# Gated delta-rule heads on one core: decay rows by DMA, tail decay on the keys, fillers in halves, a new order of a head step

## The reference

```python
mixed = silu(causal_conv(hidden @ w_qkv, conv_w))        # kernel of 4 taps
q, k, v = split(mixed)                                   # 16 key heads, 32 value heads, 128 wide
beta = sigmoid(hidden @ w_b)
g = -exp(A_log) * softplus(hidden @ w_a + dt_bias)
qf, kf = l2norm(q) * 128 ** -0.5, l2norm(k)
def step(state, t):
    state = state * exp(g_t)
    delta = (v_t - k_t @ state) * beta_t
    state = state + outer(k_t, delta)
    return state, q_t @ state
o = o * silu(z);  o = rmsnorm(o) * gamma;  return o @ w_out
```

## Time and profile before

| | us |
|---|---|
| median of 3 runs | 1450.89 |
| profiled execution, time | 1452.2 |
| profiled execution, span | 1450.4 |
| head steps (first to last state copy, 16 copies) | 102.4 to 996.8 |
| a full head step (120.67 us for two, 403.7 to 524.4) | 60.3 |
| PE busy of 119.0 us of full steps | 113.53 |
| DVE, ACT, POOL busy of the same | 93.52, 80.08, 82.18 |

### The profile page before, as it was taken

How to read it: one execution, slowest core, us unless ns; L and a number is a source line. 1 busy time by engine, 2 the same in 40 slices (tenths; PEclk the granted TensorE clock), 3 DMA queues, 4 the chain that set the end, 5 groups by cost and what they waited for, 6 DMA issues and landing times. The chain is left out here.

```text
span 1450.4 us, 24932 instructions
## 1 busy us (share of the span) xinstructions
PE 1304.9 (90%) x8680; PEld 872.4 (60%) x8680; DVE 962.6 (66%) x1918; ACT 792.2 (55%) x1944; POOL 750.8 (52%) x1245
## 2 busy tenths in 40 slices
PE   6768999999999999999999999988898899899893
PEld 4356666666666666666666666665545466545672
DVE  5847778787787877878778787774602366641454
ACT  3546676666766667666666666665432365420120
POOL 1675776857758667585676856761000000117363
PEclk9969999999999999999999999999999999999997
DMA  2534355354453544535445354364201950202687
GB/s 81 134 64 114 64 152 142 90 150 113 133 138 93 150 117 128 143 88 150 117 129 143 88 150 117 114 145 157 66 0 27 374 160 1 81 13 104 137 185 185
DMA packets 233180, 171.71 MB, mean 118 GB/s; under 512 B 163746, under 2 KB 202998, under 8 KB 230240
## 3 DMA queue, kind: packets, MB, share of 16 engines
q1 hardware_dynamic: 226912, 161.59, 41.3%
q0 software_dynamic: 6144, 8.53, 3.3%
HBM read 104.64 MB, written 65.83 MB: 118 GB/s over the span
## 5 line engine op out<-in xcount | busy, mean ns | idle before, releaser
L1267 DVE SCALAR_TENSOR_TENSOR heads_y<-psum_banks,gdn_conv_w,heads_y 128x1021 f32<-128x1021 f32 (+2 forms) x192 | 244.6, 1275 | 11.3 <-ACT heads_y L1072 6.8
L776 PE MATMUL psum_banks<-main_hT,gdn_w_in 128*128 128x512 f32 x512 | 242.6, 608 | 6.1 <-DMA gdn_w_in<-in_w_in 4.0
L1562 POOL TENSOR_TENSOR heads_XT<-heads_XT,heads_tmp 128x126 f32<-128x126 f32 (+22 forms) x496 | 205.6, 414 | 38.9
L1559 POOL TENSOR_TENSOR heads_tmp<-heads_XT,heads_A 128x126 f32<-128x126 f32 (+22 forms) x496 | 180.7, 364 | 39.8
L776 PEld LDWEIGHTS psum_banks<-main_hT,gdn_w_in 128*128 128x128 f32 x512 | 97.0, 195 | 95.8 <-issue 91.5
L1530 POOL TENSOR_TENSOR heads_og<-heads_og,heads_fac 128x512 f32<-128x512 f32 x60 | 60.5, 1039 | 138.7 <-DVE heads_fac L1333 138.7
L890 PE MATMUL psum_banks<-heads_w_z,main_hT 128*128 128x256 f32 x512 | 122.9, 383 | 0.0
L1095 ACT ACTIVATE heads_O<-psum_banks,heads_coef 128x128 f32<-128x128 f32 x224 | 69.9, 364 | 95.8 <-PE psum_banks L807 95.4
L1072 ACT ACTIVATE heads_y<-psum_banks,gdn_conv_w 128x1024 f32<-128x1024 f32 x64 | 71.4, 1116 | 89.6 <-PE psum_banks L776 89.6
L1288 DVE SCALAR_TENSOR_TENSOR heads_S<-heads_S,heads_coef,psum_banks 128x128 f32<-128x128 f32 x192 | 57.4, 340 | 85.6 <-PE psum_banks L830 85.2
L1278 DVE SCALAR_TENSOR_TENSOR heads_X<-psum_banks,heads_coef,heads_v_s 128x128 f32<-128x128 f32 x224 | 67.9, 345 | 65.3 <-PE psum_banks L805 65.3
(11 more groups left out here) (291 smaller groups left out, 2994.9 us busy)
## 6 DMA issues: line engine op xcount, KB each, us to landing
values_by_tokens<-heads_v_s SPq DMA_DIRECT2D x64, 256.0 KB, 4.1
heads_v_s<-values_by_tokens SPq DMA_DIRECT2D x16, 1024.0 KB, 5.6
outputs_by_features<-heads_ogT SPq DMA_DIRECT2D x120, 128.0 KB, 2.4
heads_ogT<-outputs_by_features SPq DMA_DIRECT2D x30, 512.0 KB, 3.7
main_w_gu<-in_w_gu SPq DMA_DIRECT2D x4, 2816.0 KB, 21.1
gdn_w_in<-in_w_in SPq DMA_DIRECT2D x16, 512.0 KB, 5.3
heads_A<-kk_blocks SPq DMA_DIRECT2D x64, 128.0 KB, 4.8
keys_by_tokens<-heads_k_tok SPq DMA_DIRECT2D x64, 128.0 KB, 3.3
```

The costliest lines, as they stand in the source:

```text
L776: ins = pe.matmul(out[:, half * 512:(half + 1) * 512], w_in[:, kd_, j * P:(j + 1) * P], hT[:, kd_, half * 512:(half + 1) * 512], start=kd_ ...
L1267: dve.scalar_tensor_tensor(y[j][:, shift:T], src[:, 0:T - shift], conv_w[:, head, j, t:t + 1], y[j][:, shift:T], ALU.mult, ALU.add).then_i ...
L1559: pool.tensor_tensor(tmp[:, 0:n, 0:m], bc_last(XT[:, 0:n, j], m), bc_mid(A0[:, j, j + 1:BLK], n), ALU.mult).then_inc(solve_step.sem, 1)
L1562: pool.tensor_tensor(XT[:, 0:n, j + 1:BLK], XT[:, 0:n, j + 1:BLK], tmp[:, 0:n, 0:m], ALU.add).then_inc(solve_step.sem, 1)
```

## The change

Four things change.

- **Decay rows.** cum is stored once in DRAM, and for each step one transfer of 1 MB (`gates`, L656 of the new code) broadcasts the 2048 values of a head to all 128 partitions, straight to `Dm`. DVE adds the mask in SBUF (`decay0` to `decay3`), ACT takes the exponential with -cum as the bias of a partition, which makes 16 instructions of 128 columns where 4 of 512 were. The 16 products on PE, both row tiles and their loads and four fills on POOL are gone. `Dm` is a single tile, so the load waits for the last `inverse` of the step before.
- **Tail decay.** ACT scales the keys instead of `Dl`: `k_tail` for chunk c+1 is written behind `Dl` of chunk c, from `k_tok`, and su becomes two products of 128 columns from `k_tail` and `Dl`.
- **Halves.** p1 to p7 (in part), z1, z2, z3, out1 and out2 can be issued in two pieces, `.0` and `.1`, in different rows.
- **Order.** All five tables of the middle steps are new.

```diff
-0: z0/0
-1: p0/-1 p1/-1
-3: z1/1
-4: z2/2 norm_q/3
-5: p2/-1
-6: decay0/3 decay1/2 decay2/0 decay3/1
...
+0: z0/3
+1: p0/-1 p1.0/-1
+2: p1.1/-1
+3: z1.0/2
+4: z1.1/2 z2.0/1
+5: z2.1/1 p2.0/-1 kk0/3
+6: norm_q/0
...
-SP_PLAN = """kt_out inverse_out kt_in inverse_in values_out products_out values_in products_in gates
-outputs_out0 outputs_in0 outputs_out1 outputs_in1 w_z w_in w_o""".split()
-POOL_PLAN = """pow q_root norm0 norm1 norm2 norm3 scale solve""".split()
+SP_PLAN = """gates inverse_out inverse_in values_out products_out values_in products_in outputs_out0 w_z outputs_in0 kt_out outputs_out1 outputs_in1 w_in kt_in w_o""".split()
+POOL_PLAN = """pow q_root norm0 norm1 norm2 scale norm3 solve""".split()
...
             def gate_rows(h):
-                for sign, rows in enumerate([row_to, row_from]):
-                    src = cum_rows[sign, IT * h:IT * (h + 1)].rearrange("(g s) t -> g s t", g=4)
-                    sp.dma_start(rows[h % 2][sign:P:32], src).then_inc(s_rows[h % 2], 16)
+                src = cum_rows[IT * h:IT * (h + 1)].rearrange("(o s) t -> o (s t)", o=1)
+                sp.dma_start(flat(Dm[:]), src.to_broadcast([P, IT * P])).then_inc(rows_in.sem, 16)
...
                 elif name == "gates":
-                    b = bank_of(h, "decay3")
-                    sp.wait_ge(full[b].sem, full[b].done(h, "decay3"))
-                    gate_rows(h + 2)
+                    sp.wait_ge(uf_ready.sem, uf_ready.end(h - 1))
+                    gate_rows(h)
...
-                        if c == 0:
-                            pe.wait_ge(kt_loaded.sem, kt_loaded.end(h - 1) * 16)
-                        pe.wait_ge(dt_ready.sem, dt_ready.done(h, f"dt{c}"))
-                        pe.matmul(flat(bank_a[:, 0:2]), k_tok[old][:, c], flat(Dt[:]), start=True, stop=True).then_inc(a_full.sem, 1)
+                        pe.wait_ge(tail_ready.sem, tail_ready.done(h, f"kt{c}"))
+                        for e in range(HD):
+                            ins = pe.matmul(bank_a[:, e], k_tail[c % 2][:, e], Dl[:, e], start=True, stop=True)
+                        ins.then_inc(a_full.sem, 1)
...
+            def tail_keys(h, c):
+                if c > 1:
+                    act.wait_ge(a_full.sem, a_full.done(h, f"su{c - 2}"))
+                elif h > 1:
+                    act.wait_ge(a_full.sem, a_full.base(h))
+                for e in range(HD):
+                    i = c * HD + e
+                    ins = act.activation(k_tail[c % 2][:, e], k_tok[(h - 1) % 2][:, c], ACT.Copy, scale=coef[:, TAIL, h - 1, i:i + 1])
+                ins.then_inc(tail_ready.sem, 1)
...
                 elif part == 1:
+                    if c == 0:
+                        act.wait_ge(kt_loaded.sem, kt_loaded.end(h - 1) * 16)
+                        tail_keys(h, 0)
                     act.wait_ge(a_full.sem, a_full.done(h, f"tx{c}"))
                     act.activation(flat(Dl[:]), flat(bank_a[:, 0:2]), ACT.Copy).then_inc(dl_ready.sem, 1)
-                    if c < C - 1:
-                        for e in range(HD):
-                            i = c * HD + e
-                            ins = act.activation(Dt[:, e], bank_a[:, e], ACT.Copy, scale=coef[:, TAIL, h - 1, i:i + 1])
-                        ins.then_inc(dt_ready.sem, 1)
+                    if c + 1 < C - 1:
+                        tail_keys(h, c + 1)
...
+                    for it in range(4 * u, 4 * u + 4):
+                        ins = act.activation(Dm[:, it], Dm[:, it], ACT.Exp, bias=coef[:, NCUM, h, it:it + 1])
...
+                if name.startswith("decay"):
+                    dve.wait_ge(rows_in.sem, rows_in.end(h) * 16)
+                    part = Dm[:, 4 * u:4 * u + 4]
+                    dve.tensor_tensor(part, part, bc_mid(limit[:], 4), ALU.add).then_inc(dm_masked.sem, 1)
+                    return
```

217 lines of the change are left out of this document (111 added, 106 removed).

## The result

| | before | after |
|---|---|---|
| median, us | 1451.25 (8 runs, 1450.56 to 1457.65) | 1440.34 (8 runs, 1435.42 to 1445.87) |
| ratio, 95% interval | | 0.9919 [0.9899, 0.9939] |
| span of the profiled execution | 1450.4 | 1441.8 |
| step 1 | 61.1 | 64.9 |
| steps 2 to 14 | 783.4 | 764.6 |

The change makes the kernel 0.8% faster: 11 us in the medians, 8.6 in the spans. I had forecast 46 us and a range of 1378 to 1438, and 1440.34 lies outside it. The sign was right, the size by far not.

What follows compares the result with a forecast made beforehand. PE, 95% busy in full steps, sets the pace, with the solve loop of POOL and SP nearly as long. Thirteen steps save 39.9 us, the others 6.0, together 45.9, giving a median of 1405; own range 1390 to 1422, whole range 1378 to 1438.

Steps and rivals of the forecast that it cites:

- two cycles of 56.0 and 56.7 us: Full steps: the POOL and SP solve loop takes 56.0 us, PE with its losses 56.7; together 57.2 a step.
- PE's floor of 54.7: PE in a full step: 57.5 us busy less 1.1 decay products and 1.7 drain; as a rival 1376, chance 0.10.
- The loop after, 56.05: Loop of POOL's solve and SP's queue after the change: a step cannot be shorter than about 56.0 us.
- speaks against the change: The solve loop of about 56.0 us, said to put PE's floor of 54.7 out of reach.
- 57.2 for a full step: Steps 2 to 14: 57.2 us each, between 56.0 and 59; 3.07 us less a step, 39.9 for thirteen.
- Decay masks: DVE's masks with both operands in SBUF hold POOL; only decay0 falls into the solve, +0.6 us on the loop.
- Exponentials: ACT: sixteen at 0.312 us for four of 0.63, +2.5 us a step as upper end, clear of Dl.
- Broadcast and tail keys: 1 MB load lands in 6.5 us against 6.4 of DVE work, no stall; tail decay on keys worth 0.
- The other steps: Outside steps 2 to 14: step 1 gains 1.5 us, steps 15 and 16 gain 2.5 and 2.0; 6.0 in all.
- Halves fill gaps: Steps 15 and 16: half fillers fill PE gaps of 0.7 to 0.9 us, worth 2.5 and 2.0 us.
- The clock: Granted clock taken as full in all but a few slices; under 1.00 in full steps was listed as a wrong sign.
- late answers: Rival: DVE and ACT answer late, fillers don't help much; 59 to 60 us a step, 1425 to 1447, chance 0.10.

Runs made afterwards that it cites:

- e18_less_pe: Changed kernel with half of the gate products' work left out, 3.45 us less PE work in each full step; 1433.41 us, ratio 0.9848 to the kernel before.
- e9_exp512: e1_old_order with four exponentials of 512 columns in place of sixteen, leaving -cum out of the decay; 1451.35 us, ratio 0.9985 to the kernel before.
- e1_old_order: Changed kernel with the middle steps' old order, without the decay products and with the broadcast first on SP; 1491.21 us, ratio 1.0265 to the kernel before.
- e7_exps_moved: e1_old_order with only the exponentials moved on ACT, to rows 8, 10, 11 and 13; 1497.86 us, ratio 1.032 to the kernel before.
- e14_dve_order: Changed kernel with two swaps on DVE, decay1 ahead of factors and tap10 ahead of turn; 1464.24 us, ratio 1.009 to the kernel before.
- e3_attn_early: Changed kernel with the product group attn0 moved ahead of y6 on PE; 1436.91 us, ratio 0.9882 to the kernel before.

## Why the prediction was wrong

The step that failed is "with two cycles of 56.0 and 56.7 us that touch at these places I take 57.2 us", for all thirteen full steps alike: it gave the inverse's round trip its usual length every time, and the granted clock as full throughout. The runs showed a code load in that round trip in every third step (60.2 us), a clock that falls behind the wait that this makes, and a second loop through `turn` and `scales` (58.0). Steps 1 and 15, which were priced from their gaps alone, failed as well.

The forecast was 45.9 us in the span, 8.6 came. The missing 37.3 us, by the steps (the rows add up to 37.2 by rounding):

| where | us | cause |
|---|---|---|
| steps 2, 5, 8, 11, 14 | 14.8 | 60.2 in the mean for 57.2: code load in the inverse's store, in three of them half clock behind it |
| the other eight full steps | 6.3 | 58.0 for 57.2: the two loops |
| step 15 | 8.7 | 56.2 for 47.5: half clock for 17 us, and gaps that were not filled |
| step 1 | 5.3 | 64.9 for 59.6: ACT waits for `A` ahead of y6's copies |
| start, step 16 and behind | 2.1 | |

Point by point:

- **PE's floor of 54.7.** That it is not to be had, and that POOL's loop forbids it, was right; `e18_less_pe` shows it. The decay products were mis-sized: with them gone and the keys scaled, a step is 0.4 us shorter in `e9_exp512`, since 0.5 of their 1.1 had covered a wait for Dl, and 0.2 are the new wait for S.
- **The loop after, 56.05.** The edit that "speaks against the change" was the right one, and it measured 58.2: landing +1.3, SP's wait for kk +1.1, decay0 0.3 less. What I didn't see is the second loop beside it, through `turn`, 15.5 us of DVE's queue and `scales`. I had read DVE's `scales` only as the wait of 1.24 us in the earlier trace rows.
- **57.2 for a full step.** The undisturbed ones take 58.0. This term failed by 0.8 us, 6.3 us over eight steps. Had nothing else been wrong, the forecast would have been inside its range.
- **Decay masks.** Right in kind. POOL's instruction takes 0.69 us beside decay0 where its neighbours take 0.38 to 0.40, +0.3 and not +0.6. The two overlap for 0.5 us, so the later one was not held in full, as I had taken it to be; and decay0 itself takes 0.80 where the other masks take 0.68, for which I had counted nothing:

```profile
346.25 0.39 POOL L1591 TENSOR_TENSOR heads_XT<-heads_XT,heads_tmp 128x108 f32<-128x108 f32 x1
346.72 0.69 POOL L1588 TENSOR_TENSOR heads_tmp<-heads_XT,heads_A 128x96 f32<-128x96 f32 x1
```

- **Exponentials.** I took 0.312 for one; it takes 0.388, and the exponentials take 2.7 us more in a step (81.0 us in all for 38.1), where 2.5 was to be the upper end. The Trainium skill ("ScalarE: Activation LUTs", "What ACT_TABLE_LOAD costs") has the difference: an operand of one value per partition adds about 93 ns. The trace roughly agrees: it has 76 ns here. That they stand clear of Dl now was right: PE's longest wait for Dl in a full step fell from 1.24 to 0.3 us. In the new order this matters little, in the old one it is all: I priced the order's worth at nothing apart from the fillers, and it is 51 us with these parts.
- **Broadcast and tail keys.** Right: 4.8 us against a cover of 6.4 (6.5 in the trace), and a ratio of 1.0 for the tail keys alone.
- **The other steps.** Failed. "Halves fill gaps", 2.5 us for step 15, was worked out from gaps alone. PE waits 5.0 us for S there (3.4 before), the granted clock is at 1.2 GHz for 17 us, and the step lost 6.2 us. At 0.4 us for each us at half clock, the price of the full steps, an estimate, the 13.7 us more make 5.6 of them. Why the clock stays low there is not shown. In step 1 the term of 1.5 us left out the wait for `A`, 6.7 us on ACT.
- **The clock.** "Nothing in the earlier trace rows foretells" a clock under 1.00: true, and still the step that failed. The earlier trace rows shows the old order, whose longest wait was 1.24 us. The new order makes one of 1.5 us ahead of y6 as soon as the inverse is late. Nothing in rows of before shows the code load either. Before, `turn` started some 22.3 us into the step, 10 to 11 us behind the issue of the inverse's load (3.8 in the change). SP and DVE in step 7 of the kernel before:

```profile
476.49 2.01 SPq L727 DMA_DIRECT2D heads_Uf<-inverse_blocks  x4
```

```profile
486.35 2.16 DVE L1322 STREAM_TRANSPOSE heads_Xh<-heads_Uf 32x512 f32<-32x512 f32 x3
```

So a late inverse cost nothing: in `e9_exp512`, in the old order, it lands 1.5 us later in steps 5 and 8, with a code load under way, than in step 7; `turn` starts 21.8 us into all three, and each takes 59.9 us. The new order calls for it at 16.7, as soon as it lands. That slack is what the change spent.

Of the rivals, "late answers" (59 to 60 us a step, 1425 to 1447, chance 0.10) holds the measured time, in good part by luck: the mean step was 58.8, and late answers are only half of the reason, the code load the other.

## What to carry to other kernels

A change that tightens an order also takes away slack that hid small disturbances: list what each wait of the new order would do if its DMA landed 1.5 us late. When an engine is busy 98%, try the loops that close over the step before believing in it; follow each from the last event of a step to the same event of the next, over every queue on the way, and add up. And price an instruction at the place where it stands: the sixteen exponentials cost 40 us in one order and hardly anything in the other.

## What the runs showed of the hardware

- Program code arrives by DMA, among the packets of the data. A 16 KB packet of kind "instruction" (0.9 to 1.6 us) in the middle of a store of 2 x 128 KB in small packets makes it land 1.5 to 1.8 us later. It recurs with the count of PE's instructions: 64 more moved it to other steps.
- In full steps the granted clock fell around the end of a wait on PE, from 0.6 us before it to 2.1 us behind, but not at every such wait: in 8 to 10 of 13 steps where it was 2.5 to 2.8 us (`e1_old_order`, `e7_exps_moved`, `e14_dve_order`), in 3 of 5 where it was 1.5 to 1.9 (the change, and there not at the two longest), in none of 5 where a wait of 1.45 to 1.58 stood elsewhere in the step (`e3_attn_early`), and where it was 1.24 in 2 of 13 (`e9_exp512`) and in none of 13 (before). 3.4 us at 1.2 GHz lengthen a step by about 1.4 us, 10.2 us by 4.3.
- An activation of 128 columns from SBUF takes 312 ns without, and 388 to 396 ns with, a scale or bias by partition.
- A step can be set by a loop over four queues while PE is busy 98% of it: 3.45 us less of PE's work changed a full step by 0.2 us (`e18_less_pe`).
